# Out projection as three products of rounded halves, with the halves made by ScalarE and GpSimd, in a two-FFN layer with a state-space mixer

## The reference

```
hidden = (Y_diag + Y_off + D * x) * silu(gate)          # 2048 x 4096, per token and channel
var    = mean(hidden * hidden)                          # over the 4096 channels
out    = (hidden * rsqrt(var + EPS) * norm_w) @ out_proj_w    # 4096 -> 256
```

## Time and profile before

| | |
|---|---|
| time, median of 3 runs | 1508.95 us (1508.79 to 1509.53) |
| the profiled execution's own time | 1511.01 us |
| its span, first to last instruction | 1509.2 us |
| mean granted TensorE clock | 0.967 of full speed |
| busy of the span: PE, DVE, ACT, POOL | 92%, 75%, 69%, 45% |
| out projections 0 to 127 | start at 345.6 us, the last ends at 1367.9 us |

### The profile page before, as it was taken

The page is one execution under the profiler, slowest core; times in us unless marked ns, Lnnn a source line. Parts: engine busy times, 40 slices in busy tenths (PEclk is TensorE's granted clock), DMA queues, the critical chain, the costliest instruction groups (busy, mean ns, idle before and its releaser), DMA issues. The chain is left out here.

```text
span 1509.2 us, 26250 instructions
## 1 busy us (share of the span) xinstructions
PE 1388.3 (92%) x8704; PEld 1091.1 (72%) x8704; DVE 1128.3 (75%) x2547; ACT 1040.4 (69%) x2133; POOL 680.6 (45%) x637
## 2 busy tenths in 40 slices
PE   4889977768999999999999999999999999986998
PEld 4878766556777777777777777777777777764787
DVE  5752444666988888897888889788888979896433
ACT  0124333576988888898888889888888988871332
POOL 1013211023656666566666656666665665661000
PEclk9999989889999999999999999999999999996999
DMA  5220000224344444343453533445444434334000
GB/s 125 71 88 25 15 15 14 69 43 102 106 105 113 123 104 114 99 107 105 110 127 100 112 98 113 103 113 122 108 108 93 116 103 112 101 95 181 15 14 28
DMA packets 102079, 136.36 MB, mean 90 GB/s; under 512 B 27744, under 2 KB 49856, under 8 KB 101824
## 3 DMA queue, kind: packets, MB, share of 16 engines
q1 hardware_dynamic: 99840, 132.67, 33.8%
q10 hardware_dynamic: 2112, 2.10, 0.4%
HBM read 124.76 MB, written 9.96 MB: 89 GB/s over the span
## 5 line engine op out<-in xcount | busy, mean ns | idle before, releaser
L843 ACT ACTIVATE M<-cum_row,cum_table 128x128 f32<-128x128 f32 x1024 | 311.8, 389 | 0.0
L1204 DVE SCALAR_TENSOR_TENSOR xs<-psum,conv_w_sb,xs 128x509 f32<-128x509 f32 (+2 forms) x384 | 284.9, 742 | 0.4
L994 POOL TENSOR_TENSOR xend<-xdt,to_end_table 128x512 f32<-128x512 f32 x128 | 148.9, 1164 | 298.1 <-DVE xdt L1215 298.1
L1592 PE MATMUL psum<-hid,wo 128*128 128x512 f32 x512 | 242.8, 596 | 9.1 <-ACT eT L754 8.8
L1000 POOL TENSOR_TENSOR hid<-hid,sg 128x512 f32<-128x512 f32 x128 | 241.8, 1889 | 0.1
L986 POOL TENSOR_TENSOR squares<-squares,sq 128x512 f32<-128x512 f32 x124 | 158.7, 1280 | 118.9 <-ACT sq L820 118.3
L1252 DVE TENSOR_TENSOR psum<-psum,e_row 128x512 f32<-128x512 f32 x128 | 89.5, 699 | 122.3 <-PE psum L1566 117.9
L1225 DVE TENSOR_TENSOR M<-M,CB 128x1024 f32<-128x1024 f32 x128 | 177.7, 1388 | 0.0
L1592 PEld LDWEIGHTS psum<-hid,wo 128*128 128x128 f32 x512 | 96.2, 189 | 84.1 <-issue 72.3
L1552 PE MATMUL psum<-xend,B_tok 128*128 128x128 f32 x1024 | 139.0, 279 | 17.5 <-POOL xend L994 17.2
L1577 PE MATMUL psum<-M,xdt 128*64 128x128 f32 x2048 | 142.7, 282 | 1.0 <-DVE psum L1252 0.9
(11 more groups left out here) (200 smaller groups left out, 3024.3 us busy)
## 6 DMA issues: line engine op xcount, KB each, us to landing
cum_row<-cum_scratch SPq DMA_DIRECT2D x256, 256.0 KB, 4.4
e_row<-e_scratch SPq DMA_DIRECT2D x256, 128.0 KB, 3.5
xw_raw<-L_attn_in_proj_w_dram SPq DMA_DIRECT2D x32, 128.0 KB, 3.0
wo_raw<-L_attn_out_proj_w_dram SPq DMA_DIRECT2D x32, 128.0 KB, 3.1
gw_raw<-L_attn_in_proj_w_dram SPq DMA_DIRECT2D x16, 256.0 KB, 6.5
x_res<-_attn_hidden_states_dram ACTq DMA_DIRECT2D x4, 512.0 KB, 9.9
x_scratch<-x_res SPq DMA_DIRECT2D x4, 512.0 KB, 2.6
x_res<-x_scratch SPq DMA_DIRECT2D x1, 2048.0 KB, 8.7
```

The costliest lines, as they stand in the source:

```text
L843: last = nc.scalar.activation(M[:, v % 3, h, c * CH:(c + 1) * CH], cum_row[:, v % 2, h, c * CH:(c + 1) * CH], ACT.Relu, bias=scalar_of(CUM ...
L994: nc.gpsimd.tensor_tensor(xend[:, v % 2], xdt[:, v % 3], per_chunk_head(TO_END, v), ALU.mult).then_inc(xend_done, 1)
L1204: nc.vector.scalar_tensor_tensor(xs[:, v % 8, shift:], psum[:, X_BANK + v % 2, 0:TT - shift], tap_of(v, step), xs[:, v % 8, shift:], ALU.m ...
L1592: last = nc.tensor.matmul(psum[:, OUT_BANK + m, :], wo[:, j, m * P:(m + 1) * P], hid[:, v % 2, :], start=(j == 0), stop=(j == GP - 1))
```

## The change

`out_proj` becomes a `split_matmul` on halves of `wo` and of `hid`. Therefore:

- ACT makes `hid_hi` (a copy rounded to float32r) ahead of each square. For the slot after a silu slot, high half and square are done already in the silu slot, between the relus and the exponentials.
- POOL makes `hid_lo = hid - hid_hi` as the first thing of each slot, after it has waited for high half and square; then follow `add_squares`, `to_chunk_end` and `gate` as before.
- The weights `wo` are scaled in place in `wo_raw`, then copied to `wo_hi` by ACT, and POOL makes `wo_lo`; the last of a group in slot 1 rather than 0. The second half of the gate weights `gw` is split in slot 9 rather than 8, and has one raw buffer for the two halves.
- To make room in SBUF: `xend` and `e_row` have one buffer, `load_e` loads for slot s+3, and the zero state is gone: for tile 0 the first chunk's scan is a copy of the product, the first of the four `off` products is left out, and `scale_off` works on 384 columns.

```
@@ scalar
-                nc.scalar.activation(wo[:, p % GP, :], wo_raw[:, p % 2, :], ACT.Copy,
-                                     scale=norm_sb[:, p:p + 1]).then_inc(wo_done, 1)
+                nc.scalar.activation(wo_raw[:, p % 2, :], wo_raw[:, p % 2, :], ACT.Copy,
+                                     scale=norm_sb[:, p:p + 1]).then_inc(wo_done, 1)
+                if p >= GP:
                     act.wait_ge(out_done, nth(last_of(p - GP)))
+                act.wait_ge(wo_done, p + 1)
+                nc.scalar.activation(wo_hi[:, p % GP, :], wo_raw[:, p % 2, :], ACT.Copy).then_inc(wo_hi_done, 1)
+            def hid_to_hi(v):
+                act.wait_ge(hid_done, nth(v))
+                act.wait_ge(out_done, nth(v - 2))
+                nc.scalar.activation(hid_hi[:, v % 2, :], hid[:, v % 2, :], ACT.Copy).then_inc(hid_hi_done, 1)
...
-                if alive(s):
+                if alive(s) and (s < 0 or s % GP != 1):
+                    hid_to_hi(s)
                     square(s)
...
+                if s >= 0 and s % GP == 0:
+                    hid_to_hi(s + 1)
+                    square(s + 1)
                 if alive(s + 3):
                     exps(s + 3)
...
-                if g < GROUPS - 1 and u in (6, 8):
-                    split_g_hi(2 * (g + 1) + u // 2 - 3)
+                if g < GROUPS - 1 and u in (6, 9):
+                    split_g_hi(2 * (g + 1) + u // 3 - 2)
...
-                if g > 0 and u == 0:
+                if g > 0 and u == 1:
                     scale_wo(g * GP + GP - 1)
@@ gpsimd
+            def split_wo_lo(p):
+                pool.wait_ge(wo_hi_done, p + 1)
+                if p >= GP:
+                    pool.wait_ge(out_done, nth(last_of(p - GP)))
+                nc.gpsimd.tensor_tensor(wo_lo[:, p % GP, :], wo_raw[:, p % 2, :], wo_hi[:, p % GP, :].bitcast(F32),
+                                        ALU.subtract).then_inc(wo_lo_done, 1)
+            def hid_to_lo(v):
+                pool.wait_ge(hid_hi_done, nth(v))
+                pool.wait_ge(sq_done, nth(v))
+                nc.gpsimd.tensor_tensor(hid_lo[:, v % 2, :], hid[:, v % 2, :], hid_hi[:, v % 2, :].bitcast(F32),
+                                        ALU.subtract).then_inc(hid_lo_done, 1)
...
-                pool.wait_ge(states_done, nth(v - 2))
+                pool.wait_ge(states_done, nth(v - 1))
...
                 if alive(s):
+                    hid_to_lo(s)
                     add_squares(s)
...
+                if g > 0 and u == 1:
+                    split_wo_lo(g * GP + GP - 1)
...
-                if u in (6, 8):
-                    split_g_lo(2 * (g + 1) + u // 2 - 3)
+                if u in (6, 9):
+                    split_g_lo(2 * (g + 1) + u // 3 - 2)
...
+                if u >= 13:
+                    split_wo_lo((g + 1) * GP + u - 13)
@@ sync
-                sp.wait_ge(off_scaled, nth(v - 2))
+                sp.wait_ge(off_scaled, nth(v - 1))
...
-                if alive(s + 4):
-                    load_e(s + 4)
+                if alive(s + 3):
+                    load_e(s + 3)
@@ vector
+                if chunk == 0:
+                    nc.vector.tensor_copy(inner[:, v % 2, 0].rearrange("p h q -> p (h q)"),
+                                          psum[:, ST_BANK, 0:P]).then_inc(scan_step, 1)
+                    return
...
-                dve.wait_ge(e_in[v % 2], (v // 2 + 1) * 32)
-                nc.vector.tensor_tensor(bank(Y_BANK), bank(Y_BANK), e_row[:, v % 2, :], ALU.mult).then_inc(off_scaled, 1)
+                dve.wait_ge(e_in, (v + 1) * 32)
+                cols = slice(CH if at_slot(v)[1] == 0 else 0, TT)
+                nc.vector.tensor_tensor(psum[:, Y_BANK, cols], psum[:, Y_BANK, cols], e_row[:, cols],
+                                        ALU.mult).then_inc(off_scaled, 1)
...
-                dve.wait_ge(sq_done, nth(v - 2))
@@ tensor
-                for c in range(CPT):
-                    if c > 0:
-                        before = inner[:, v % 2, c - 1]
-                    else:
-                        before = zero_state[:] if t == 0 else carry[:, t % 2, j]
+                first = 1 if t == 0 else 0
+                for c in range(first, CPT):
+                    before = inner[:, v % 2, c - 1] if c > 0 else carry[:, t % 2, j]
...
-                pe.wait_ge(hid_done, nth(v))
-                pe.wait_ge(wo_done, pair_of(v) + 1)
+                pe.wait_ge(hid_hi_done, nth(v))
+                pe.wait_ge(hid_lo_done, nth(v))
+                pe.wait_ge(wo_lo_done, pair_of(v) + 1)
...
-                    last = nc.tensor.matmul(psum[:, OUT_BANK + m, :], wo[:, j, m * P:(m + 1) * P], hid[:, v % 2, :],
-                                            start=(j == 0), stop=(j == GP - 1))
+                    cols = slice(m * P, (m + 1) * P)
+                    last = split_matmul(nc, psum[:, OUT_BANK + m, :], wo_hi[:, j, cols], wo_lo[:, j, cols],
+                                        hid_hi[:, v % 2, :], hid_lo[:, v % 2, :], start=(j == 0), stop=(j == GP - 1))
```

More of the change, by code:

```diff
@@ L401, in macaron @@
     wo_raw = sb("wo_raw", [P, 2, D], F32)
-    wo = sb("wo", [P, GP, D], F32)
+    under, sbu = scope()
+    w_bc_raw = sbu("w_bc_raw", [P, KT, 2 * N], F32)
+    w_dt_raw = sbu("w_dt_raw", [P, KT, H], F32)
+    under.close()
+    wo_hi = sb("wo_hi", [P, GP, D], F32R)
+    wo_lo = sb("wo_lo", [P, GP, D], F32R)
     under, sb = scope()
@@ L430, in macaron @@
     M = sb("M", [P, 3, 2, TT], F32)
-    e_row = sb("e_row", [P, 2, TT], F32)
+    e_row = sb("e_row", [P, TT], F32)
     xdt = sb("xdt", [P, 3, CPT, 2, HP], F32)
-    xend = sb("xend", [P, 2, CPT, 2, HP], F32)
+    xend = sb("xend", [P, CPT, 2, HP], F32)
     inner = sb("inner", [P, 2, CPT - 1, 2, HP], F32)
     carry = sb("carry", [P, 2, GP, 2, HP], F32)
-    hid = sb("hid", [P, 2, TT], F32)
+    hid_hi = sb("hid_hi", [P, 2, TT], F32R)
+    under, sbu = scope()
+    hid = sbu("hid", [P, 2, TT], F32)
+    under.close()
+    hid_lo = sb("hid_lo", [P, 2, TT], F32R)
     sq = sb("sq", [P, TT], F32)
-    zero_state = sb("zero_state", [P, 2, HP], F32)
     halo = sb("halo", [P, 2, GP, TAPS - 1], F32)
@@ L504, in scans @@
         g, u = divmod(v, SLOTS)
-        return g * 120 + 8 * u - 2 * max(u - 12, 0) + 2 * c + h + 1
+        t = u // GP
+        earlier = g * (GP * (7 + 8 + 8 + 6)) + 8 * u - min(u, GP) - 2 * max(u - 3 * GP, 0)
+        return earlier + (max(2 * c + h, 1) if t == 0 else 2 * c + h + 1)
     def sums_before(v):
@@ L692, in split_g_hi @@
                     act.wait_ge(g_proj, nth(last_of(2 * q + 1 - GP)))
[L693 removed]
+                nc.scalar.activation(gw_hi[:, :, cols], gw_raw[:], ACT.Copy).then_inc(gw_hi_done, 1)
             def scale_wo(p):
@@ L1242, in scan @@
                     else:
-                        before = zero_state[:, h, :] if t == 0 else carry[:, t % 2, j, h, :]
+                        before = carry[:, t % 2, j, h, :]
                     after = carry[:, (t + 1) % 2, j, h, :] if c == CPT - 1 else inner[:, v % 2, c, h, :]
@@ L1552, in states @@
                     last = nc.tensor.matmul(psum[:, ST_BANK, c * P:(c + 1) * P], B_tok[:, t * CPT + c, :],
-                                            xend[:, v % 2, c].rearrange("p h q -> p (h q)"), start=True, stop=True)
+                                            xend[:, c].rearrange("p h q -> p (h q)"), start=True, stop=True)
                 last.then_inc(states_done, 1)
@@ L1567, in off @@
                                             before.rearrange("p h q -> p (h q)"), CT[:, tok:tok + CH],
-                                            start=(c == 0), stop=False, skip_group_check=True)
+                                            start=(c == first), stop=False, skip_group_check=True)
                 last.then_inc(off_done, 1)
```

67 lines of the change are left out of this document (31 added, 36 removed).

## The result

The changed kernel takes **1556.62 us** (median, 1555.67 to 1558.56), the kernel before 1509.01 in the same comparison: ratio **1.032, 95% interval [1.030, 1.033]**. The forecast was 1498, with a range of 1480 to 1518.

A forecast was written before the change was run, and what follows sets the result against it. PE was taken to set the pace, with ACT and DVE close behind. Seven groups -21, half the last -1, last slots +8.8 and head +1.6 gave -11.6 us: 1498, range 1480 to 1518 (8 in 10).

The forecast's parts named there:

- The slots with weights: Slots 8 to 11 of a group: 33.9 us in all, with a 1.5 us wait in slot 10 and 0.5 for clock.
- The tie: POOL's `xend` against DVE's mask behind silu slots: `xend` first only in slots 4 and 5, 15.8 us; other pairs about 16.55.
- The `wo` halves: Weight halves of the out projection: about 2.5 us a group on ACT for `wo_hi`, four low halves on POOL.
- ACT and POOL become the bound: Rival: the loop over both engines carries its lateness into the next silu slot; group 132.8 us, 1528 in all, chance 0.20.
- the plain slot: PE, from out projection to out projection: 7.64 us, 0.31 less than before.
- the silu slots: First slot of every four on PE: 8.15 us, with `off` behind DVE.
- a last slot: End of the loop, without projections: 7.0 us a slot, +1.76 each over five slots, +8.8 in all.
- the head: Start of the loop: ACT's slot 0 gets more work ahead of `eT`, so the first out projection waits +1.6 us.
- The early half: High half and square made ahead of the silu slot's exponentials: the earlier square pays for the low half, and no more.
- ACT's load: ACT's busy time per group: from 113.9 to 124.7 us.
- The rival of `e_row`: Rival: late `e_row` loads hold `scale_off` and `diag`, 1 us in one slot of sixteen, 8 us: 1506, chance 0.06.
- The sum: Whole kernel: -21 for seven groups, -1 for half the last, +8.8 last slots, +1.6 head: -11.6 us.

The follow-up runs named there:

- d1: c1 with the load of pair 2's x weights issued one slot earlier, slot 6 and not 7: 1524.3 us, ratio 1.008 to the kernel before.
- b3: The changed kernel with the square made from `hid_hi`, so `hid_lo` need not wait for it: 1545.3 us, ratio 1.022 to the kernel before.
- c2: c1 with b3's edit, the square made from the high half: 1549.6 us, ratio 1.025 to the kernel before.
- c1: The changed kernel with x weights halved in slots 6, 7, 7, 10 and `gw`'s second high half in slot 8, loads unmoved: 1564.3 us.
- e2: d2 without b3's edit, the square back on `hid` and `hid_lo` waiting for it: 1514.5 us, ratio 1.002 to the kernel before.
- d2: c3 with d1's earlier load of x weights and b1's order of loads: 1501.2 us, ratio 0.993 to the kernel before.
- c3: c2 with `wo` halves in slots 14, 15, 15 and 2 instead of 13, 14, 15 and 1: 1542.3 us, ratio 1.020 to the kernel before.
- a3: The changed kernel with high half and square of the slot behind the silu slot made after the exponentials: 1586.0 us, ratio 1.050 to the kernel before.
- b1: The changed kernel with the load of `e_row` ahead of that of `cum_row` on SP's queue: 1556.6 us, ratio 1.029 to the kernel before.
- e1: d2 without b1's edit, the load of `e_row` back behind that of `cum_row`: 1501.9 us, ratio 0.995 to the kernel before.

## Why the prediction was wrong

- **"The slots with weights" failed**, and it is the largest part. The step followed `gw`'s second half through slots 9 and 10 and counted every other weight half as 0.2 us on POOL, with the sentence that weight halves "stand behind `gate` and lie in the time in which POOL waits for ACT". For slot 8 that is false: there the half waits for the end of ACT's silu slot, and the new `hid_lo` is queued behind it. Slot 9 was forecast at about 8.5 and took 14.4; with the queue mended (d1) the four slots take 33.4 us, against 33.9 forecast. Worth 4.8 us a group, 32 us of the 58.6 between forecast and result. For the slower clock behind a wait the step kept 0.5 us; it took 2.1 of the 5.9. The wait that it did foresee, 1.5 us for `gw_lo` in slot 10, did not come: no product of the projections waits in the loop.
- **The tie failed, in its order and number, not in its rule.** The rule (who starts first runs, the other stands) held in all 128 `xend` of the kernel after; the order did not, in slot 5 by 0.05 us, since `xend` started 14.55 into the silu slot and not 14.44. That is 0.9 us on the pair of slots 4 and 5. Slots 2 and 14 had gone into the sum as plain slots and took 1.1 and 1.3 us more each: a second tie there was not seen. Behind both stands `hid_lo`'s wait for the square: without it slots 1, 5 and 13 fall to 7.6 and slots 2 and 14 grow, in all 11.3 us less alone, 14.7 and 13.3 with the queue mended in part or in full (b3, c2 against c1, e2 against d2). How much of that is the tie and how much the 0.6 us itself wasn't separated.
- **The `wo` halves were put in ACT's total and not on a path.** In slots 1 and 13 their 0.95 us stand ahead of the next high half, behind a silu slot that is late already. Moving them was worth 7.3 us (c3 against c2).
- **The rival "ACT and POOL become the bound" was the nearest**, at 1528 with a chance of 0.20, and right only in part. That the loop of ACT and POOL is late behind a silu slot is what slots 1, 2, 5, 13 and 14 show. But it catches up: slots 3, 7 and 11 take 7.6 to 7.7 us, and the next silu slot begins on time, where the rival had the lateness carried on. It had 1.2 us a group above the kernel before; measured are 5.0, of which 4.8 are the queue of slot 9, which it did not know. With the queue mended (d1) a group is 131.8, below its 132.8.
- **Right:** the plain slot (7.61, forecast 7.64), the silu slots (slot 0 shorter, 7.61), a last slot at 7.07, +1.7 at the head, and about right the exponential's start in the silu slot (forecast 13.1 us into it; 13.1 to 13.4 in group 4's slots 0, 4 and 12, 13.9 in slot 8). The early half is a gain, as a3 shows, though the prediction claimed only that it pays for the low half. ACT's load was forecast at 124.7 us a group; by the same sum it is 266.75 / 300 of 136.6 = 121.5 in the changed kernel and 124.6 in d2.
- **The rival of `e_row` is refused twice** (b1, e1): DVE waits for it, and mending that changes the time by nothing that can be told.
- The sum: at slot 0 of the last group the kernel after is 35.0 us behind the one before, and the last group and what stands behind it add 12.6. The forecast had -19.4 there (-21 for seven groups, +1.6 at the head), and +7.8 behind it. So nearly all of the miss is in the seven groups, where the terms above lie.

What stays open: the last group was not taken apart, and its last slots take 6.49 us in d2, where they took 5.23 before. PE waits for `hid_lo` ahead of all six products, though four of them don't use it; another order was not tried. And no run has one buffer of `e_row` in the kernel before.

## What to carry to other kernels

An instruction that nobody waits for may stand anywhere in an in-order queue; as soon as the next engine waits for something queued behind it, write out that queue for every slot, with what each entry waits for, above all in the slots whose producer is late. When work is moved, its load moves too. And a named wait is no price: removing `e_row`'s 36 us of waits gained nothing, removing a 0.6 us wait for a square gained 11 to 15. Last, when repairs make a changed kernel win, give the old kernel the repairs that it can share before the change gets the credit.
